# Attention and feed-forward on one core: the last four heads taken by halves of the batch, feed-forward of the first half beside attention of the second

## The reference

```python
# x (8, 128, 512), ctx (8, 128, 512), 32 heads of 128, eps 1e-5, 8 experts' scales
h = layernorm(x)
q = (rmsnorm(h) * ln_w) @ w_q.T;  k = ctx @ w_k.T;  v = ctx @ w_v.T      # to (8, 128, 32, 128)
s = einsum("bqhd,bkhd->bhqk", q, k) + position_bias                       # no scaling by sqrt(d)
p = softmax(where(mask, s, -inf), -1)
x = x + h + einsum("bhqk,bkhd->bqhd", p, v).reshape(8, 128, 4096) @ w_out.T
n = layernorm(x)
routing = softmax(n @ gate_w.T)                                           # (tokens, 8)
f = (n * (routing @ in_scale)) @ sign(weight).T * (routing @ out_scale) + bias
return x + n + f
```

## Time and profile before

| what | us |
|---|---|
| median of 3 runs | 896.69 (894.68 to 901.8) |
| the profiled execution | 896.83 |
| its span, first to last instruction | 894.7 |
| TensorE busy in it | 846.8 |
| DVE, ACT, POOL busy in it | 647.4, 380.6, 291.4 |
| mean granted clock of TensorE | 0.982 |

### The profile page before, as it was taken

The page is one execution under the profiler, slowest core; times in us unless marked ns, Lnnn a source line. Parts: engine busy times, 40 slices in busy tenths (PEclk is TensorE's granted clock), DMA queues, the critical chain, the costliest instruction groups (busy, mean ns, idle before and its releaser), DMA issues.

```text
span 894.7 us, 12797 instructions
## 1 busy us (share of the span) xinstructions
PE 846.8 (95%) x4302; PEld 703.3 (79%) x4302; DVE 647.4 (72%) x1039; ACT 380.6 (43%) x987; POOL 291.4 (33%) x283
## 2 busy tenths in 40 slices
PE   5699999999999998799999999999999999978798
PEld 4588888888778877688888888888888888867575
DVE  5966756756887597777777777767786777667785
ACT  4422422422432353355544554455445544543452
POOL 4021111111021023344445544545355435421242
PEclk9899999999999999999999999999999999999988
DMA  7163463463554547342143214421442144220002
GB/s 246 71 216 126 153 216 126 153 215 127 171 184 146 197 136 256 134 144 95 56 148 144 100 52 148 145 97 55 148 144 96 55 148 145 77 93 29 1 4 91
DMA packets 57376, 113.80 MB, mean 127 GB/s; under 512 B 5065, under 2 KB 33865, under 8 KB 52065
## 3 DMA queue, kind: packets, MB, share of 16 engines
q1 hardware_dynamic: 57312, 112.99, 36.7%
HBM read 77.32 MB, written 35.65 MB: 126 GB/s over the span
## 4 chain that ended last, share of the span: by engine, by line
PE 79%; DVE 11%; ACT 3%; DMA 3%; issue 2%; POOL 1%; SPq 0%; DVEq 0%; ACTq 0%; POOLq 0%
PE out L1058 10%; PE out L1060 9%; PE out L1059 9%; PE proj L1058 8%; PE proj L1060 8%; PE proj L1059 8%; PE o L1130 7%; PE s L1111 6%; PE t L1119 3%; PE s L1058 3%; PE s L1059 3%; PE s L1060 3%; DVE w_lo L788 2%; DMA w_stage<-in_wq 2%; DMA w_stage<-in_wk 1%
## 5 line engine op out<-in xcount | busy, mean ns | idle before, releaser
L690 ACT ACTIVATE probs<-probs,neg_max 128x128 f32<-128x128 f32 x256 | 99.8, 391 | 162.4 <-DVE neg_max L915 162.4
L560 POOL TENSOR_TENSOR w_stage<-w_stage 128x256 f32<-128x256 f32 x32 | 25.1, 786 | 346.6 <-DMA w_stage<-in_wk 279.4
L939 DVE TENSOR_TENSOR acc<-out,acc 128x512 f32<-128x512 f32 x128 | 87.6, 688 | 46.6 <-PE out L1060 45.7
L1058 PE MATMUL out<-wo_hi,o_hi 128*128 128x512 f32 x256 | 110.5, 432 | 6.0 <-POOL wo_lo L587 3.7
L572 POOL TENSOR_TENSOR w_lo<-w_stage,w_hi 128x512 fp32r<-128x512 f32 (+1 forms) x52 | 59.1, 1148 | 135.6 <-ACT w_hi L637 135.6
L1060 PE MATMUL out<-wo_lo,o_hi 128*128 128x512 f32 x256 | 101.9, 398 | 0.0
L1059 PE MATMUL out<-wo_hi,o_lo 128*128 128x512 f32 x256 | 101.2, 395 | 0.0
L1058 PE MATMUL proj<-x_hi,w_hi 128*128 128x512 f32 x210 | 88.6, 422 | 2.6 <-DVE w_lo L788 1.6
L637 ACT ACTIVATE w_hi<-w_stage 128x512 fp32r<-128x512 f32 (+1 forms) x120 | 65.9, 566 | 43.6 <-POOL w_stage L562 32.2
L1060 PE MATMUL proj<-x_lo,w_hi 128*128 128x512 f32 x210 | 82.6, 393 | 0.0
L1059 PE MATMUL proj<-x_hi,w_lo 128*128 128x512 f32 x210 | 82.1, 391 | 0.0
(11 more groups left out here) (201 smaller groups left out, 2058.6 us busy)
## 6 DMA issues: line engine op xcount, KB each, us to landing
k_spill<-ring SPq DMA_DIRECT2D x64, 256.0 KB, 2.9
v_spill<-ring SPq DMA_DIRECT2D x64, 256.0 KB, 2.2
w_stage<-in_wk SPq DMA_DIRECT2D x32, 256.0 KB, 3.0
big_stage<-in_wv SPq DMA_DIRECT2D x8, 1024.0 KB, 8.0
w_stage<-in_wq SPq DMA_DIRECT2D x32, 256.0 KB, 4.1
k_first<-k_spill SPq DMA_DIRECT2D x8, 1024.0 KB, 7.1
v_first<-v_spill SPq DMA_DIRECT2D x8, 1024.0 KB, 4.9
k_second<-k_spill SPq DMA_DIRECT2D x8, 1024.0 KB, 6.5
```

What stands on the lines that cost most here:

```text
L690: last = act.activation(probs[:, j % 2, b, :], probs[:, j % 2, b, :], ACT.Exp, bias=neg_max[:, col:col + 1], accum_out=row_sum[:, col:col ...
L939: dve.tensor_tensor(acc[:, b, :], out_bank[n % 2][:], acc[:, b, :], ALU.add).then_inc(v_acc, 1)
L1058: pe.matmul(to[:], left_hi, right_hi, start=first and n == 0, stop=False, skip_group_check=True)
```

## The change

Heads 28 to 31 are taken half by half: units 56 to 59 are these four heads with the first half of the batch, 60 to 63 the same with the second. Their position biases are loaded twice (four more loads of 64 KB). The output weights of pairs 14 and 15 get tiles of their own in memory that the query products have left. The output products of these pairs, the signs, the scales, statistics, transposes and the first two routers get new places, the tail a new order. The tiles of the feed-forward part move to other memory, its transposes, router and input scales of the first half to the banks `proj0` and `proj1`. The arithmetic is the same.

```diff
+SPLIT = NH - 4
+UNITS = [(h, half) for h in range(SPLIT) for half in range(2)] + [(h, half) for half in range(2) for h in range(SPLIT, NH)]
+BIASES = list(range(SPLIT)) + 2 * list(range(SPLIT, NH))
+
+def bias_of(j):
+    return j // 2 if j < 2 * SPLIT else j - SPLIT
...
+        load = []
+        if 1 <= bias_of(j + 2) < len(BIASES) - 2 and bias_of(j + 2) != bias_of(j + 3):
+            load = [("BL", bias_of(j + 2) + 2)]
...
-        else:
-            o = p - 1
-            steps += [("SIGN", c) for c in range(2)]
-            steps += slot(j, outs(o, 3, 4), outs(o, 5), [], [("SIGN", 2)])
-            steps += slot(j + 1, outs(o, 6), outs(o, 7), [("WO", p)], [("SIGN", 3), ("SCALES",)])
-            steps += slot(j + 2, outs(p, 0), outs(p, 1), [])
-            steps += [("ST", 0), ("ST", 1)]
-            steps += slot(j + 3, outs(p, 2), outs(p, 3), [])
-            steps += [("ST", 2), ("ST", 3), ("LN2", 0)]
-    steps += [("NT", 0), ("NT", 1), ("OUT", p, 4), ("ST", 4), ("TX", 0), ("TX", 1), ("NT", 2), ("NT", 3), ("OUT", p, 5),
-              ("G", 0), ("ST", 5), ("TX", 2), ("TX", 3), ("ROUTE", 0), ("OUT", p, 6), ("RT", 0), ("RTC", 0), ("ST", 6), ("G", 1),
-              ("R", 0), ("ROUTE", 1), ("RTC", 1), ("Y", 0), ("OUT", p, 7), ("YL", 0), ("RT", 1), ("ST", 7), ("R", 1), ("OS", 0),
-              ("LN2", 1), ("NT", 4), ("NT", 5), ("Y", 1), ("NT", 6), ("NT", 7), ("M", 0), ("OS", 1), ("M", 1), ("TX", 4), ("TX", 5),
-              ("YL", 1), ("G", 2), ("ROUTE", 2), ("TX", 6), ("TX", 7), ("OS", 2), ("M", 2), ("RT", 2), ("RTC", 2), ("G", 3), ("R", 2),
-              ("OS", 3), ("Y", 2), ("YL", 2), ("ROUTE", 3), ("M", 3), ("OS", 4), ("M", 4), ("RT", 3), ("RTC", 3), ("OS", 5), ("R", 3),
-              ("Y", 3), ("YL", 3), ("M", 5), ("OS", 6), ("M", 6), ("OS", 7), ("M", 7)]
+    j = 2 * SPLIT
+    a, b, c = SPLIT // 2 - 1, SPLIT // 2, SPLIT // 2 + 1
+    steps += [("FW",)]
+    steps += slot(j, outs(a, 3), outs(a, 4), [], [("WO", b), ("SIGN", 0), ("WOL", c)])
+    steps += slot(j + 1, [], outs(a, 5), [], [("SIGN", 1), ("WO", c)])
+    steps += slot(j + 2, outs(b, 0), outs(b, 1, 2, 3), [], [("SIGN", 2)])
+    steps += slot(j + 3, outs(a, 6), outs(a, 7), [], [("SIGN", 3), ("SCALES",)])
+    steps += slot(j + 4, [], outs(c, 0, 1), [], [])
+    steps += slot(j + 5, outs(c, 2), outs(c, 3), [], [("ST", 0), ("ST", 1)])
+    steps += slot(j + 6, outs(b, 4, 5) + [("ST", 2), ("ST", 3), ("LN2", 0)], outs(b, 6, 7), [("NT", 2), ("NT", 3)], [("NT", 0), ("NT", 1)])
+    steps += slot(j + 7, [("TX", 0), ("TX", 1)], [("TX", 2), ("TX", 3)], [("G", 0), ("G", 1)])
+
+    steps += [*outs(c, 4), ("ST", 4), ("ROUTE", 0), *outs(c, 5), ("RT", 0), ("RTC", 0), ("ST", 5), ("ROUTE", 1), *outs(c, 6), ("ST", 6),
+              ("R", 0), ("RT", 1), ("RTC", 1), *outs(c, 7), ("ST", 7), ("LN2", 1), ("Y", 0), ("R", 1), ("YL", 0), ("OS", 0), ("OS", 1),
+              ("NT", 4), ("NT", 5), ("M", 0), ("TX", 4), ("TX", 5), ("Y", 1), ("NT", 6), ("NT", 7), ("M", 1), ("G", 2), ("YL", 1),
+              ("TX", 6), ("TX", 7), ("ROUTE", 2), ("OS", 2), ("M", 2), ("G", 3), ("RT", 2), ("RTC", 2), ("ROUTE", 3), ("OS", 3), ("R", 2),
+              ("M", 3), ("RT", 3), ("RTC", 3), ("Y", 2), ("YL", 2), ("OS", 4), ("R", 3), ("OS", 5), ("M", 4), ("Y", 3), ("YL", 3), ("M", 5),
+              ("OS", 6), ("M", 6), ("OS", 7), ("M", 7)]
...
-        y_tiles = [w_stage[:, 2 * k:2 * k + 2].rearrange("p h t -> p (h t)") for k in range(2)]
-        res_tiles = w_stage[:, 4:8].rearrange("p (r h) t -> p r (h t)", h=2)
+        nt_tiles = ffn_raw
+        y_tiles = [wo_raw[:, k] for k in range(2)]
+        res_tiles = k_first[:, 0].rearrange("p (r n) -> p r n", r=2)
-        n_tiles = ring[:, (NKV + LAST - 1) % 3]
-        nt_tiles = k_first[:].rearrange("p h (r n) -> p (h r) n", r=2)
+        n_tiles = ffn_neg
...
+        def output_tiles(p):
+            if p == SPLIT // 2:
+                return [tiles[:, 0:4].rearrange("p (k a) t -> p k (a t)", a=2) for tiles in (w_hi, w_lo)]
+            if p == SPLIT // 2 + 1:
+                return x_lo[:, 5], x_lo[:, 6]
+            return wo_hi[:], wo_lo[:]
+        def ffn_bank(i):
+            return proj_bank[i % 2] if i < HALF else s_bank[i % 2]
+        def gate_bank(p):
+            return proj_bank[p] if p < 2 else t_bank
+        def in_scale_bank(p, k):
+            return proj_bank[k] if p == 0 else (o_bank, s_bank[1])[k]
...
-            def ffn_weights(c):
-                if c == 0:
-                    for part in range(4):
-                        sp.wait_ge(*low_done(2 * NPAIR - 1, part))
-                    sp.dma_start(ffn_raw, ffn_w).then_inc(d_ffn_w, 16)
+            def ffn_weights():
+                for part in range(4):
+                    sp.wait_ge(*low_done(2 * NPAIR - 1, part))
+                sp.dma_start(ffn_raw, ffn_w).then_inc(d_ffn_w, 16)
...
-                if p:
+                if p >= SPLIT // 2:
+                    act.wait_ge(pe_prod, 7 * len(GROUPS))
+                elif p:
                     act.wait_ge(pe_out, max(nth_out[p - 1, b] for b in range(B)))
-                act.activation(wo_hi[:], wo_raw[:], ACT.Copy).then_inc(a_wo_hi, 1)
+                act.activation(output_tiles(p)[0], wo_raw[:], ACT.Copy).then_inc(a_wo_hi, 1)
```

More of the change, by code:

```diff
@@ L67 @@
 LAST = NPAIR - 1
-UNITS = [(h, half) for h in range(NH - 2) for half in range(2)] + [(NH - 2, 0), (NH - 1, 0), (NH - 2, 1), (NH - 1, 1)]
+SPLIT = NH - 4
[3 more added lines that the diff above has]
+    return j // 2 if j < 2 * SPLIT else j - SPLIT
 def schedule():
@@ L197, in schedule @@
     q = at[QUERIES[0]]
-    for p in range(NPAIR):
+    for p in range(SPLIT // 2):
         j = 4 * p
         n = q + p + 2
-        has = n < len(GROUPS)
-        prod = {i: product(n, i) if has else [] for i in SLOT}
+        prod = {i: product(n, i) for i in SLOT}
         m = NPAIR + p + 2
-        def split(*parts):
-            return [("WX", m, part) for part in parts] if has else []
+        load, sums = [], []
+        if n + 1 < len(GROUPS):
+            load = [("WL", m + 1, 0), ("WL", m + 1, 1)]
+            sums = [("WS", m + 1), ("WX", m + 1, 0)]
@@ L1136, in output @@
                 n = nth_out[p, b]
+                tiles = output_tiles(p)
                 pe.wait_ge(g_wo_lo, p + 1)
@@ L1140, in output @@
                 toks = slice(b * P, (b + 1) * P)
-                three(to, [(both((o_hi, o_lo), everything, k, toks), both((wo_hi, wo_lo), everything, k, everything))
+                three(to, [(both((o_hi, o_lo), everything, k, toks), both(tiles, everything, k, everything))
                            for k in range(2)], pe_out)
```

58 lines of the change are left out of this document (26 added, 32 removed).

## The result

The changed kernel takes 908.58 us (median of 4 runs, 905.46 to 911.04) against 895.68 for the kernel before in the same series (894.54 to 901.8): ratio 1.0128, 95% interval 1.0071 to 1.0185. It is slower by 1.3%, and the forecast was 901.5 with a range up to 907. The profiled execution has a span of 905.9 us against 894.7.

A forecast was written before the change was run, and what follows sets the result against it. TensorE, busy for 95% of the span, was taken as the bound, with only the last 110 us open to change. Stretches of +3.3, -2.5 and +4.0 on a 894.7 us span gave 899.5, hence 901.5 us; range 891 to 907.

The forecast's parts named there:

- S57: Start of the scores of unit 57, where the schedules first differ; taken as 784.56 us in both kernels.
- stretch 1: From the scores of unit 57 to those of unit 63: 46.0 us against 42.69, +3.3.
- stretch 2: From the scores of unit 63 to the end of the last output product: 28.4 us against 30.91, -2.5.
- stretch 3: From the last output product to the last matmul: 36.2 us against 32.23, +4.0, including +1.7 for low clock.
- SIGN 0: Slot 56: two VectorE operations on feed-forward weights, held by POOL's weight subtraction and mask sum, cost 2.9 us.
- SCALES: Slot 59: scale split on VectorE delays pair 15's output products and unit 61's mask add to 2.3 us after their scores.
- rival D: Low clock decides, in slots 57 to 61 and the waits of stretch 3: 908 us; chance 0.13.
- A: Slot 56: VectorE reaches SIGN 0 ahead of POOL, 2.9 us less, 898.6 us; chance 0.15.
- B: No wait replaces those removed; stretch 1 is 36.2 us, the sum 9.8 lower, 891.7 us; chance 0.18.
- C: The first half's feed-forward part fills every wait, last stretch as dense as before's (32.2): 885.7 us; chance 0.09.

The follow-up runs named there:

- e1: Changed kernel with pair 14's output weights split behind the values of unit 56, not ahead of them; 905.06 us, ratio to before 1.0067 to 1.0147.
- e4: Kernel before with own tiles for pair 15's output weights, split in slot 60 ahead of the values; 898.32 us.
- e9: Changed kernel with the first scaling left behind the last output product and before's order from the second scaling on; 898.22 us.
- e2: Changed kernel with the first scaling ahead of the last output product again and before's order from there on; 897.78 us, ratio to before 1.0006.
- e3: Changed kernel with the split of the experts' scales early in slot 58 instead of slot 59; 909.61 us.
- e10: Changed kernel with one step moved: the second scaling goes ahead of product 0; 905.79 us.
- e12: Changed kernel plus 14 unread matmuls on TensorE in the 3.58 us pause ahead of product 0; 905.99 us.
- e7: Changed kernel with only the tail's head in before's order: first scaling ahead of the last output product, second out-scale behind product 0; 902.13 us.
- e5: Changed kernel with e1, e2 and e3 together; 895.76 us, ratio to before 0.9970 to 1.0009.
- e8: e5 with the split of pair 15's output weights moved from slot 57 to slot 58; 894.51 us, ratio to before 0.9976.
- e6: Kernel before with own tiles for pair 15's output weights, split in slot 60 behind the values; 894.48 us, ratio 0.9962 to 0.9994.
- e11: e6 with the split of the scales moved early in its slot; 896.02 us, ratio to before 0.9992.

## Why the prediction was wrong, step by step

**Start and sum.** 901.5 was 899.5 of span and 2.0 around it. The measured 905.9 comes from it as 1.67 (S57, scatter) + 1.46 (stretch 1) - 1.2 (stretch 2) + 4.9 (stretch 3) - 0.4 (after the last matmul). Only stretch 3 is an error of size. The median of 908.58 lies 0.6 above the profiled execution's 907.99. (The forecast calls an OUT a head's product; its 1.38 us are six matmuls, the product of a pair.)

**SIGN 0: right.** Forecast held by 2.9 us; measured 3.73 for the two operations against 1.12 free, so 2.6. The data came at 792.55, 6.3 behind S57, as forecast (790.3 to 791 on its clock); its own sum, 2.1 MB at 393 GB/s from 784.4, would give 789.7. From S57 on its end was forecast at 10.3 us and came at 10.1, the values of unit 57 at 14.4 (14.2), the scores of unit 60 at 25.3 (25.5). The Trainium skill, page SBUF — State Buffer, section "SBUF: two separate sides", names an exclusive lock that is held for the whole instruction; this trace agrees (2.21 beside 2.54 us of POOL), and so do e1 and e4.

**SCALES: right.** The mask add of unit 61 was forecast 820.3 - 816.95 = 3.35 us after the start of its scores. Behind SCALES and the low half it came at 822.06, 3.15 after 818.91; in slot 57 of before it came 792.97 - 791.88 = 1.09 after the earlier trace rows:

```profile
820.21 1.22 DVE L1005 TENSOR_TENSOR x_lo<-scales_raw,x_lo 8x1024 fp32r<-8x1024 f32 x1
821.45 0.69 DVE L960 TENSOR_TENSOR o_lo<-o,o_hi 128x512 fp32r<-128x512 f32 x1
822.06 0.68 DVE L943 TENSOR_TENSOR probs<-s,bias_mask 128x512 f32<-128x512 f32 x1
```

The OUTs of slot 60 then ran at low clock, which the sum had not: that slot took 8.64 us, not 7.75, and it makes most of stretch 1's 1.46. The forecast of 46.0 lies inside the 45.69 to 47.68 of the six executions with the same steps.

**Stretch 2: right.** Forecast 28.4, measured 27.16 and 26.87 to 27.62 in the six. The wait for the weights is gone as said.

**Stretch 3: the step that failed is its charge for the low clock.** The prediction's sum at full clock was 34.5: 7.95 us of idle time (3.55 + 1.8 + 0.6 + 1.6 + 0.4) and 26.55 of work. The measured idle time is 8.09. That agreement is partly luck: product 2 waited 0.89, not 1.8, and no bank is named for which the transposes (1.22) and the input scales (0.62) waited. Work at full clock was 33.05 - 5.5 = 27.6, 1.0 more than counted; before's rows give 31.03 - 3.9 = 27.2 for the same steps. The rest, 3.8 us, is the clock: the text took "one more spell than before's two", that is three, and then added 1.7 us. That is about the price of a single spell by its own figure of 1.6 in rival D, and less than before had lost to its two, half of 7.7, which is 3.9. Three spells are 4.8 us at 1.6 each and 5.8 at before's rate, or 3.9 with the third hidden in waits that the text assumed; they cost 5.5. With 3.9 to 5.8 in place of 1.7, stretch 3 would have come out at 38.4 to 40.3 and the time at 903.7 to 905.6, up to the bound of 1%, so the 0.17 for slower was too low. The measured 908.58 would still have been above it. The range up to 907 was laid around the charge that was too low. What the order behind the first scaling costs is 5.8 us of the stretch (e9), 4.4 as waits and 1.4 as clock.

**The rivals.** A (DVE first at SIGN 0) didn't happen: DVE waited 0.31 us for the data and POOL was ahead. B and C fell by their own signs (scores of unit 63 at 833.69, first product 5.20 after the last OUT). D named the right mechanism, too many spells of low clock, and the waits of stretch 3 as one of its places. Its 908 is near the measured time by luck, since it was worked out from half clock through slots 59 and 60; there it didn't come (stretch 1 has 0.89, its mark was 0.85). It was given 0.13.

**What is shown and what isn't.** Shown by undoing: the tail's order makes the slowdown (e2, e9); SIGN 0's delay is POOL's subtraction (e1); SCALES delays slot 60 (e3). Shown too: neither the bank wait of 1.22 us (e10) nor the pause of 3.58 (e12) is the cause by itself; the other waits weren't undone one by one. Between the changed kernel and e9 the medians differ by 10.4 us and the stretches by 5.8 + 1.4 + 0.3; the rest may be the scatter of the profiled executions and of four runs, which isn't shown. Open: why TensorE's clock falls where it does. The sum of half clock in stretches 2 and 3 is 16.7 to 17.3 us in all six versions with the new order behind product 0 (changed, e1, e3, e7, e10, e12), while its places differ; so the 0.80 of e1 and e3 looks like a spell moved out of stretch 2. It is 7.0 to 10.6 in the four variants of the changed kernel with before's order there (e2, e5, e8, e9). But before has 13.3 and e6 and e11 have 16.5 with that order, so the order alone doesn't set it. (The clock is rounded to 0.01, which is up to 0.4 us in one such stretch.)

## What to carry to other kernels

When an order of steps is rewritten for one place, the steps behind it should keep the old distance between a result of VectorE or ScalarE and the TensorE step that needs it: here before's order behind product 0 hid 4.1 of 4.5 us of waits, and nothing of the work had changed. Price every spell of low clock that the sum assumes, each one, check that the total isn't below what the kernel before pays for fewer spells, and if a sum has several times the idle time of before, let the range reach up to the next spell. A transfer of work to GpSimd, or a place for it, is chosen by what VectorE does beside it: the same subtraction made stretch 1 4.1 us longer beside operations on two SBUF tiles (e4) and no longer beside reads of PSUM (e6).
